# Down products of the first expert placed ahead of the router's gates in three mixtures of experts

## What is computed

```python
# L0_ffn: a shared expert and eight routed ones, hidden 512, tanh-Gelu
shared = new_gelu(xf @ Wfc_s + bfc_s) @ Wproj_s + bproj_s
probs = jax.nn.softmax(xf @ Wr, axis=-1)
topk_p, topk_i = jax.lax.top_k(probs, 2);  topk_p = topk_p / jnp.sum(topk_p, ...)
for e in range(8): routed += (new_gelu(xf @ Wfc[e] + bfc[e]) @ Wproj[e] + bproj[e]) * gate[:, e:e+1]
return shared + routed
# L1_ffn: eight experts, hidden 256, gated by SiLU
h0 = x @ w0[e].T + b0[e];  h1 = x @ w1[e].T + b1[e]
out[e] = (h0 * silu(h1)) @ w2[e].T + b2[e];  result = sum of softmax(top-2 logits) * out[top-2]
# L3_ffn (its last part): eight experts, hidden 512, erf-Gelu, gates = softmax of the top-2 probabilities
acc = acc + (gelu(out1 @ We1[e] + be1[e]) @ We2[e] + be2[e]) * gate
```

## Time and profile before

| what | value |
|---|---|
| median of three runs | 5651.73 us |
| the profiled execution | 5653.67 us |
| its span | 5652.1 us |
| mean granted TensorE clock | 0.983 of full |
| PE busy | 5157.4 us (91%) |
| DVE busy | 2826.8 us (50%) |
| ACT busy | 2968.7 us (53%) |
| GpSimd busy | 411.3 us (7%) |
| HBM traffic | 14 GB/s over the span |

### The profile page before, as it was taken

The page is one execution under the profiler, slowest core; times in us unless marked ns, Lnnn a source line. Parts: engine busy times, 40 slices in busy tenths (PEclk is TensorE's granted clock), DMA queues, the critical chain, the costliest instruction groups (busy, mean ns, idle before and its releaser), DMA issues. The chain is left out here.

```text
span 5652.1 us, 82883 instructions
## 1 busy us (share of the span) xinstructions
PE 5157.4 (91%) x29024; PEld 2646.7 (47%) x29024; DVE 2826.8 (50%) x6586; ACT 2968.7 (53%) x10228; POOL 411.3 (7%) x930
## 2 busy tenths in 40 slices
PE   7999999989899999998989999999898999989989
PEld 4444444554444444555444444455544444445553
DVE  5255555562525555556252555555625255555562
ACT  5444565564544446556454444655645444465564
POOL 0000101110000010211000001021100000102110
PEclk9999999999999999999999999999999999999999
DMA  1100000000010000000001000000000100000000
GB/s 37 41 6 6 18 18 12 5 1 15 25 41 6 6 18 18 12 5 1 17 23 41 6 6 19 20 9 5 1 17 23 41 6 6 23 16 9 5 1 19
DMA packets 22513, 86.01 MB, mean 15 GB/s; under 512 B 2512, under 2 KB 3024, under 8 KB 21968
## 3 DMA queue, kind: packets, MB, share of 16 engines
q1 hardware_dynamic: 22096, 80.58, 4.4%
HBM read 78.47 MB, written 2.10 MB: 14 GB/s over the span
## 5 line engine op out<-in xcount | busy, mean ns | idle before, releaser
L1115 ACT ACTIVATE work<-bank,rowmax 128x128 f32<-128x128 f32 (+1 forms) x3072 | 1063.5, 399 | 190.1 <-DVE rowmax L1428 190.1
L573 PE MATMUL bank<-mask_causal,identb 128*128 128x512 bf16 x2940 | 816.7, 389 | 43.0 <-issue 28.6
L1428 DVE TENSOR_REDUCE rowmax<-bank 128x4 f32<-128x512 f32 (+2 forms) x1152 | 608.7, 578 | 431.0 <-PE bank L725 314.8
L742 PE MATMUL bank<-ident,work 128*128 128x128 f32 (+1 forms) x4096 | 628.1, 279 | 149.8 <-DVE probsT L1489 114.6
L1115 ACT ACTIVATION_READ_ACCUMULATOR work<-bank,rowmax 128x1 f32 x3072 | 755.3, 246 | 0.0
L742 PEld LDWEIGHTS bank<-ident,work 128*128 128x128 f32 (+1 forms) x4096 | 473.4, 142 | 365.5 <-DVE probsT L1489 188.3
L1226 ACT ACTIVATE work<-bank,small 128x512 f32<-128x512 f32 x544 | 371.2, 688 | 479.0 <-PE bank L938 478.5
L965 PE MATMUL bank<-work,slot 128*128 128x512 f32 x1344 | 611.8, 592 | 0.0
L1685 DVE SCALAR_TENSOR_TENSOR part<-bank,small,sq 128x512 f32<-128x512 f32 x192 | 144.1, 751 | 794.7 <-PE bank L965 784.8
L1489 DVE COPY probsT<-bank 128x512 f32<-128x512 f32 (+2 forms) x832 | 475.6, 600 | 50.6 <-PE bank L742 44.5
L1762 POOL TENSOR_TENSOR ptmp<-work 128x512 f32<-128x512 f32 (+1 forms) x128 | 127.7, 998 | 5002.6 <-ACT work L1113 4940.6
(11 more groups left out here) (287 smaller groups left out, 6955.9 us busy)
## 6 DMA issues: line engine op xcount, KB each, us to landing
slot<-in_w_stream SPq DMA_DIRECT2D x68, 512.0 KB, 3.3
slot<-in_w_stream SPq DMA_DIRECT2D x32, 768.0 KB, 3.9
slot<-in_w_stream SPq DMA_DIRECT2D x32, 384.0 KB, 3.0
small<-in_w_small SPq DMA_DIRECT2D x1, 2288.0 KB, 8.7
x<-in_x SPq DMA_DIRECT2D x8, 256.0 KB, 3.6
out<-x SPq DMA_DIRECT2D x8, 256.0 KB, 2.0
ctx<-in_ctx SPq DMA_DIRECT2D x8, 77.0 KB, 3.5
```

What stands on the lines that cost most here:

```text
L573: nc.tensor.matmul(b[:], identb[:], mask["causal"][:].unsqueeze(1).to_broadcast([P, 4, P]), start=True, stop=True)
L742: ins = nc.tensor.transpose(b[0:nk, j * P:(j + 1) * P], probs[t % 2][:, r, j, 0:nk], ident[:])
L1115: ins = nc.scalar.activation(out, raw, ACT.Exp, bias=top, accum_out=expsum[t % 2][:, 4 * r + j:4 * r + j + 1])
L1428: V.tensor_reduce(m[:, 4 * r:4 * r + J], banks.where(("scores", n, c, s, r))[:, 0:J * nk] .rearrange("p (j k) -> p j k", j=J), AX_X, ALU.m ...
```

## The change

In `down`, the spread of the gates becomes a function of its own, `spread_gate`. On PE, at i = 1, down(0,0) follows up(0,1) directly, without fillers, transposes or a spread ahead of it. At i = 2, after up(1,0), come the transposes (with 3 fillers behind the first bank wait), and, where no expert is shared, both spreads of expert 0 and then down(0,1); where one is shared, down(0,1) comes ahead of the transposes. From i = 3 the order is as before. The 3 or 6 fillers at i = 1 and the 29 of the gated mixture are gone. On ACT the tanh of the gates moves behind the activations of (0,1), and the gate copies of (0,0) and (0,1) are both made at i = 2 (`gates_at`). On DVE `gated(0,0)` moves ahead of chain 1's search, and the copies to `gateT` and the first combines move from i = 1 to i = 2, behind `gated(1,0)`; the shared expert's combines stay at i = 1 and 2.

```diff
+        def gates_at(st, i):
+            work_items = [(e, c) for e in range(EXPERTS + st["shared"]) for c in C]
+            if st["shared"]:
+                return work_items[i - 1:i] if i > 2 else []
+            return work_items[0:2] if i == 2 else work_items[i - 1:i] if i > 2 else []
...
                         def gate_rows(c):
-                            b = bank(("gate_rows", n, c), ("gateT", (n, c)))[:].bitcast(BF16)
+                            b = bank(("gate_rows", n, c), ("gateT", (n, c)))
+                            if c == 0:
+                                fill(b, 3)
+                            b = b[:].bitcast(BF16)
                             pe.wait_ge(*have("gate", (n, c)))
...
+                        def spread_gate(e, c):
+                            b = bank(("gate_wide", n, e, c), ("gate_copy", (n, e, c)))
+                            if e == st["shared"]:
+                                pe.wait_ge(*have("gateT", (n, c)))
+                            nc.tensor.matmul(b[:, 0:TOK], gpick[:, e - st["shared"]], gateT[c][:], start=True,
+                                             stop=True).then_inc(*made("gate_wide", (n, e, c)))
...
                             if i == 1:
-                                warm(6 if st["on"] == "probs" else 3)
+                                down(*work_items[0])
+                            if i == 2:
+                                if st["shared"]:
+                                    down(*work_items[1])
                                 for c in C:
                                     gate_rows(c)
-                                if st["glu"]:
-                                    warm(29)
-                            if i:
+                                if not st["shared"]:
+                                    for c in C:
+                                        spread_gate(0, c)
+                                    down(*work_items[1])
+                            if i > 2:
+                                spread_gate(*work_items[i - 1])
                                 down(*work_items[i - 1])
...
                             if i == len(work_items):
                                 tables(common)
                                 step(then)
-                            if i:
-                                e, c = work_items[i - 1]
-                                if st["shared"] and e == 0:
-                                    continue
+                            for e, c in gates_at(st, i):
                                 act.wait_ge(*have("gate_wide", (n, e, c)))
...
                                 link(V.tensor_tensor(T[0], T[0], bc(k[7]), ALU.mult))
+                            if c and st["glu"]:
+                                gated(0, 0)
...
                         for i in range(len(work_items) + 1):
-                            if i < len(work_items) and st["glu"]:
+                            if 0 < i < len(work_items) and st["glu"]:
                                 gated(*work_items[i])
-                            if i == 1:
+                            if i == 2:
                                 for c in C:
                                     dve.wait_ge(*have("gate_rows", (n, c)))
                                     V.tensor_copy(gateT[c][0:3 * EXPERTS], banks.where(("gate_rows", n, c))[:].bitcast(BF16)
                                                   [0:3 * EXPERTS, 0:TOK]).then_inc(*made("gateT", (n, c)))
-                            if i:
+                            for e, c in gates_at(st, i):
+                                combine(e, c)
+                            if st["shared"] and i in (1, 2):
                                 combine(*work_items[i - 1])
```

More of the change, by code:

```diff
@@ L1228, in moe @@
                                                              ).then_inc(*made("hid", (n, e, c, m)))
+                            if i == 1:
+                                for c in C:
+                                    act.wait_ge(*have("gate_gap", (n, c)))
+                                    nc.scalar.activation(gcol[c][:, 6], gcol[c][:, 6], ACT.Tanh, scale=0.5
+                                                         ).then_inc(*made("gate_tanh", (n, c)))
                             if i == len(work_items):
@@ L1625, in moe, with gated @@
                         desc = W("descending").unsqueeze(1).to_broadcast(wide)
+                        E = EXPERTS + st["shared"]
+                        work_items = [(e, c) for e in range(E) for c in C]
+                        def gated(e, c):
+                            for m in range(2):
+                                b = banks.where(("hid_raw", n, e, c, m))[:, 0:TOK]
+                                dve.wait_ge(*have("silu", (n, e, c, m)))
+                                dve.wait_ge(*have("hid_raw", (n, e, c, m)))
+                                V.scalar_tensor_tensor(hid[c][:, m, :], b, W(base + "_b0")[:, 2 * e + m:2 * e + m + 1],
+                                                       silu[c][m][:], ALU.add, ALU.mult).then_inc(*made("gated", (n, e, c, m)))
                         for c in C:
@@ L1664, in moe @@
                             ins.then_inc(*made("gate", (n, c)))
[L1665 to L1674, removed]
                         def combine(e, c):
```

## The result

The median before was 5652.94 us (5650.98 to 5657.88, five runs), after it is 5628.58 us (5621.80 to 5636.29, five runs): a ratio of 0.9951, with a 95% interval of 0.9940 to 0.9963. So the change makes the kernel faster by 24 us, where 41 were forecast, and the median lies above the range's end of 5623. The profiled execution after took 5622.36; the one before took 5653.67, so the pair that can be compared line by line differs by 31.3 us.

What follows compares the result with a forecast made beforehand. PE, busy 91% of the span, was taken to bound the kernel. Savings of 46.4 (gated), 0 (last) and 1.3 (shared) less 6.8 for clock falls gave 40.9 us: from the median 5651.73 to 5611, range 5599 to 5623.

Steps and rivals of the forecast that it cites:

- What bounds the kernel: Whole span: TensorE (PE) is busy 91%, so only its idle time, fillers or half-clock time can be gained.
- Gated mixture: up(0,1) to up(1,1): 26.41 us becomes 14.8, saving 11.6 a round, 46.4 in all, at whole clock.
- the wait of 0.2 for the bank of (0,1,0): Gated mixture: PE ends up(1,0) at 640.0 and waits 0.2 us for the bank, free at 640.2.
- Last mixture: Second spread at 1303.9 against 1303.88 before: 0.0 saved, between 0.5 gained and 0.5 lost.
- Shared mixture: The second transpose's wait goes: 0.33 us saved a round, 1.3 in four.
- A fall behind the new idle stretches: Gated and last mixtures: half clock behind new waits, 1.7 us each, four of eight starts, 6.8 us lost.
- strict reading: Gated and last mixtures: by the skill's section every start would pay for a clock fall, 13.6 us instead of 6.8.
- After which both kernels do the same work in the same order: From the start of up(1,1) in a mixture, work and order were taken as unchanged.
- The falls elsewhere: Outside the changed stretches: a shift can move the 15 old falls; 3 more or fewer are 5 us.
- Rival 2: Gated and last mixtures: the clock falls in all eight starts, 34.1 us saved, 5618; chance 0.18.
- The local terms and the ring: Mixtures: gated 46.4, last 0, shared 1.3 us saved; the changed turn of banks behind them was not forecast.
- The range: Total time: 5599 to 5623 us, allowing 5 us for moved old falls.

Runs made afterwards that it cites:

- after with the second fillers: The changed kernel plus fillers in the bank of the waiting instruction, ahead of its wait, in PE's idle stretches: 5586.87 us, ratio to before 0.9874.
- the one with the take: The changed kernel with one more bank taken, and no filler put into it, in the shared mixture: 5638.65 us, ratio to before 0.9962.
- those with 53 and 27 fillers: The changed kernel with 53 or 27 fillers ahead of down(0,1) of each gated mixture: 5652.03 us (0.9984) and 5640.21 us (0.9970).
- either set of fillers in the idle stretches: The changed kernel with fillers meant for idle stretches: first set, partly ahead of chain 0, 5663.06 us; second, in the waiting instruction's bank, 5586.87 us.
- the first pair of filled kernels: Longer warm calls ahead of chain 0 and more fillers in the last attention steps: 5663.06 us on the changed kernel, 5713.65 on before.

## Why the prediction was wrong, point by point

- *What bounds the kernel:* right, as far as the runs go. All eleven experiments moved PE's idle time, fillers or clock, and the total followed; none makes another engine alone faster.
- *Gated mixture:* right. 14.92 us against 14.8; the waits 1.01 and 1.54 against 1.1 and 1.6; the wait of 0.2 for the bank of (0,1,0) did not show. Two small misses cancel in it: the waits came to 2.55 us instead of 2.9, and the rest to 12.37 instead of 11.9.
- *Last mixture:* 0.16 us lost against 0.0, within the 0.5 allowed. *Shared mixture:* 0.32 to 0.35 us against 0.33.
- *A fall behind the new idle stretches:* 1.7 us each is right (after with the second fillers: 96.0 us for the gated stage, with its fall; after in round 1: 94.33, without). The count was not: two of eight in the profiled execution after, rounds 2 and 4 of the gated mixture, and none in the last mixture, so 3.4 us and not 6.8. Round 2:

```profile
2044.35 0.38 PE L965 MATMUL bank<-gateT,gpick 128*128 128x512 bf16 x1 [1.02 <-DVE gateT L1714]
2046.27 0.61 PE L965 MATMUL bank<-gateT,gpick 128*128 128x512 bf16 x1 [1.54 <-DVE part L1700]
2046.66 3.18 PE L975 MATMUL bank<-work,slot 128*128 128x512 f32 x4
```

  Four records take 3.18 us, against 1.88 with their end at whole clock. The last mixture's pair, 0.37 and 1.54, never fell, in none of the 24 starts of the six kernels that have both waits (after, the one with the take, those with 53 and 27 fillers, and the new order with either set of fillers in the idle stretches). The gated pair, 1.01 and 1.54, fell in 16 of 24: 2 of 4 in after, 4 of 4 with the second fillers, 0 of 4 with the first, 2 of 4 with the take, 4 of 4 with 53 and with 27. (In four of these traces the first spread's record is missing, and the pairs read as one wait, 2.94 in the gated mixture and 2.29 in the last.) The section of the Trainium skill that the prediction weighed (TensorE: Matmul & The Clock Gate, "A second HAM failure mode: psum-queue depth-cycling") tells of a kernel whose clock swings because PE stands idle briefly between groups of matmuls; this case's traces agree for the gated pair in part and for the last mixture's not at all, so the prediction's strict reading of it, a fall at every start, does not hold.
- *"After which both kernels do the same work in the same order":* the first step that failed. The order was the same, the banks were not; 14 to 16 us of gain were overlooked. This error lies on the side of a faster kernel, and hid a part of the next one.
- *The falls elsewhere:* the step that put the time outside the range, a term that was mis-sized. Rival 2 named the mechanism and gave it 5 us either way, as if some 15 falls could move by three. The local terms and the ring, 46.0 + 1.4 - 0.6 + 14 to 16, come to 61 to 63 us of gain; 31.3 were measured in the profiled pair. So falls, the new ones included, took 30 to 31 us net, where 6.8 were forecast and 5 either way allowed. The half-clock time bears this out: 228 us after against the 163 of before that remain without its four stops, 65 us more, which is 32 us lost at half speed. Two things made it small. The count of single idle stretches near 2 us with a fall went only from 15 of 36 to 18 of 32, but falls behind shorter and double ones had not been counted, and in all the profile has 35 separate stretches at half clock in place of 27. And in the cross attention one fall costs 3.8 us (10 us at half clock), not 1.7.
- *The range:* its ends were made from one profiled execution. The five runs of after span 15 us, and the ten with 27 fillers 40. The scatter that the falls bring belonged into it: the three shown of before, within 2 us, hid it. That the profiled execution after, 5622.36, lies inside the range is luck.

Open: what decides whether a given idle stretch is followed by a fall. It is not its length alone (2.17 us did and did not, in the same place), nor the order of the work. That fillers in the gated mixture alone change the clock of the whole kernel is shown with 53 of them (0.982 to 0.984 against 0.977 to 0.980), and the falls that went lie in the linear part, over 300 us behind them. That speaks for the shift in time, but no run shifts the kernel without adding matmuls; and why the shift of the change itself was a bad one is not known. Nor was it tried to fill every idle stretch.

## What to carry to other kernels

Removing a filler or a dummy step that takes a buffer from a ring is a change of everything behind it: compare both kernels stage by stage between fixed rows before calling the rest unchanged. Where the engine's clock falls behind short idle stretches, a local gain is known well and the total is not: put that scatter into the range, and put fillers into the very bank of the instruction that waits, ahead of its wait. A filler one instruction too early costs its full time and cures nothing, as the first pair of filled kernels shows. Profile more than one execution where executions differ by more than the effect in question, and run the kernel to compare with beside the others each time.

## What the runs showed of the chip

- The clock fell behind single idle stretches of PE of only 2.0 to 2.4 us, in 15 of 36 cases before and in 18 of 32 after, and in the same place in one execution and not in another, with the same program up to there (122.58 and 123.70). Behind a pair of 0.4 and 1.0 us it fell in all four rounds of after with the second fillers.
- The price of a fall goes with what PE does behind it: 1.7 us in a dense stretch of matmuls, 3.8 us in the cross attention, where PE kept 10 us at 1.2 GHz.
- Fillers of 1.9 us in an idle stretch of 2.17 held the clock there in every round of the three kernels that have them (19.96 us for the first cross attention each time). The scatter of executions was 5 us over four runs with them and 15 over five without on after, but still 18 over ten on before.
